# Attention's output kept as channel rows through HBM and divided per eight heads, with two expert weight loads moved into routing

## What is computed

```python
# layer 0, attention: 16 heads of width 16
Q, K, V = (proj(Wq, bq), proj(Wk, bk), proj(Wv, bv))         # [4, 16, 1024, 16]
scores = jnp.einsum('bhqd,bhkd->bhqk', Q, K) * scale
attn = softmax(scores, axis=-1)
out = jnp.einsum('bhqk,bhkd->bhqd', attn, V)
out = out.transpose(0, 2, 1, 3).reshape(B, S, D) @ Wo.T + bo
x = layernorm(x + out)
# layer 0, experts: top 2 of 8 by softmax(x @ w_gate.T), hidden width 1024
h = gelu(einsum('td,edh->teh', flat_x, W1) + b1)
y = einsum('teh,ehd->ted', h, W2) + b2
x = layernorm(x + sum of the two chosen experts, weighted)
```

## Time and profile before

| | us |
|---|---|
| median of 3 runs | 2013.42 (2012.56 to 2052.93) |
| the profiled execution, its own time | 2010.89 |
| its span, first to last instruction | 2008.9 |
| attention's loop over heads | about 104 to 897 |
| output projection | 899 to 942 |
| normalisation, gate, routing | 942 to 1015 |
| experts of layer 0 | 1016 to about 1580 |
| second layer | from about 1590 |

### The profile page before, as it was taken

The page is one execution under the profiler, slowest core; times in us unless marked ns, Lnnn a source line. Parts: engine busy times, 40 slices in busy tenths (PEclk is TensorE's granted clock), DMA queues, the critical chain, the costliest instruction groups (busy, mean ns, idle before and its releaser), DMA issues. The chain is left out here.

```text
span 2008.9 us, 36274 instructions
## 1 busy us (share of the span) xinstructions
PE 1763.1 (88%) x11202; PEld 1122.9 (56%) x11203; DVE 1146.1 (57%) x2473; ACT 887.8 (44%) x1306; POOL 408.6 (20%) x573
## 2 busy tenths in 40 slices
PE   7999999999999999988479999999999579944772
PEld 4523444444444444437368888888888546943551
DVE  4688888888888888846821111111111287797223
ACT  3436666666666666664112333333332144230223
POOL 2310000000000000003013333333333100000782
PEclk9969999999999999999789999999999879977896
DMA  5501111111111111106624443344344300024544
GB/s 196 181 18 36 36 32 32 32 32 34 35 34 32 32 32 33 35 23 201 228 86 117 101 116 104 109 110 110 111 105 114 93 6 1 2 84 147 87 54 168
DMA packets 101160, 157.44 MB, mean 78 GB/s; under 512 B 19984, under 2 KB 76624, under 8 KB 95728
## 3 DMA queue, kind: packets, MB, share of 16 engines
q1 hardware_dynamic: 70720, 120.30, 18.4%
q0 software_dynamic: 21696, 23.85, 7.5%
q10 hardware_dynamic: 8688, 12.58, 1.7%
HBM read 122.23 MB, written 48.37 MB: 85 GB/s over the span
## 5 line engine op out<-in xcount | busy, mean ns | idle before, releaser
L552 DVE TENSOR_REDUCE unit_max<-ps_ring 128x1 f32<-128x512 f32 x1024 | 639.3, 683 | 70.1 <-PE ps_ring L427 64.1
L538 ACT ACTIVATE w<-ps_scores 128x1024 f32<-128x1024 f32 x512 | 503.6, 1022 | 263.3 <-PE ps_scores L504 260.4
L427 PE MATMUL ps_ring<-k_stack,q_stack 96*128 96x512 bf16 x1024 | 367.6, 393 | 17.6 <-POOL v_padded L390 7.6
L504 PE MATMUL ps_scores<-q_stack,k_stack 98*128 98x512 bf16 x1024 | 307.5, 382 | 2.6 <-ACT w L538 2.5
L1486 PE MATMUL m_ps_h<-m_xt,m_w 128*128 128x256 f32 x1248 | 278.6, 382 | 0.8 <-DVE m_xt L1537 0.8
L1498 PE MATMUL m_ps_y<-w,m_ht 128*128 x1248 | 275.8, 379 | 0.0
L449 PE MATMUL ps_o<-w,v_padded 128*32 128x256 f32 x4096 | 261.9, 385 | 0.0
L1486 PEld LDWEIGHTS m_ps_h<-m_xt,m_w 128*128 128x128 f32 x1248 | 239.0, 192 | 34.2 <-DVE m_xt L1537 1.2
L1498 PEld LDWEIGHTS m_ps_y<-w,m_ht 128*128 128x128 f32 x1248 | 234.2, 190 | 30.3
L427 PEld LDWEIGHTS ps_ring<-k_stack,q_stack 96*128 96x128 bf16 x1024 | 98.8, 97 | 259.0 <-DVE unit_max L552 177.2
L1518 ACT ACTIVATE m_ht<-m_ps_h,m_w 128x256 f32<-128x256 f32 x312 | 130.7, 470 | 144.8 <-PE m_ps_h L1486 144.8
(11 more groups left out here) (263 smaller groups left out, 1624.2 us busy)
## 6 DMA issues: line engine op xcount, KB each, us to landing
m_w<-in_w SPq DMA_DIRECT2D x39, 1028.0 KB
rows<-g_rows SPq DMA_DIRECT2D x16, 512.0 KB, 3.0
y<-sums SPq DMA_DIRECT2D x16, 512.0 KB, 7.1
q_parts<-qk_part SPq DMA_DIRECT2D x16, 384.0 KB
k_parts<-qk_part SPq DMA_DIRECT2D x16, 384.0 KB
q_stack<-q_parts SPq DMA_DIRECT2D x64, 96.0 KB
k_stack<-k_parts SPq DMA_DIRECT2D x64, 96.0 KB
xt<-in_xt ACTq DMA_DIRECT2D x8, 512.0 KB, 10.0
```

Source lines behind the costliest of these rows:

```text
L427: nc.tensor.matmul(out[:, :], qs[0:STACK, u, qt * P:(qt + 1) * P], ks[0:STACK, u, half * HALF:(half + 1) * HALF], start=True, stop=True).t ...
L504: mm = nc.tensor.matmul(p_s[kt % 2][:, half * HALF:(half + 1) * HALF], ks[:, u, kt * P:(kt + 1) * P], qs[:, u, half * HALF:(half + 1) * HALF],
L538: nc.scalar.activation(pt[:, kt, :], p_s[kt % 2][:, :], ACT.Exp, scale=SCALE)\
L552: nc.vector.tensor_reduce(unit_max[:, u % 2, half, qt:qt + 1], src[:, :], axis=AX.X, op=ALU.max).then_inc(ring_used, 1)
```

## The change

1. In attention the fold is gone: no transposes back, no `normalise`, no `c.ao`. Each head's `o_transposed` (32 rows of 1024 queries) is stored to `o_raw` in HBM by SP (`store_o`, 128 KB). Before ACT writes `o_transposed` for head n it waits until the store of head n - 2 has landed.
2. Heads are grouped by eight: the first and last groups are written out, six between are a hardware loop. Per group, one group late, SP loads the raw rows of eight heads (512 KB) and their sums (`load_block`, at head 1), DVE takes 64 reciprocals per partition (after head 2), SP stores them to HBM (at head 3) and reads them back spread over the 16 channels of each head (512 KB, at head 4), and DVE multiplies 128 x 1024 values (`scale_block`, after head 5) into `c.o_t`, channels on partitions. At the end of each group two ring numbers are passed over, to keep the loop's bank numbers fixed.
3. The output weights, the bias and the tokens of sequence 0 are loaded near the end of attention, and POOL adds the bias to those tokens there.
4. `stage_output` reads `c.o_t` directly as the stationary operand: no staging, transposes or copies; four PSUM banks in place of two, four token buffers in place of two. The last block of eight heads is loaded, inverted, stored, loaded back and scaled in this stage, in DVE's list the reciprocal ahead of the first pair and the scaling ahead of pair 5; only pairs 12 to 15 need it.
5. The first weights of expert units 0 and 1 are loaded by SP in routing, as soon as DVE has the owners of the units (L1144), behind the copies to `sums`.

```diff
+def load_block(sp, c, g):
+    raw = c.o_raw[bass.ds(g * HEADS, HEADS), :, :]
+    sp.dma_start(c.raw[:, :, :].rearrange("p j f -> p (j f)"), raw[:, 0:HD, :]).then_inc(c.raw_loaded, 16)
+    sp.dma_start(c.den[:, :], raw[:, HD, :]).then_inc(c.den_loaded, 16)
+def store_reciprocals(sp, c, g):
+    sp.dma_start(c.o_inv[bass.ds(g, 1), :].rearrange("a (p f) -> (a p) f", p=P), c.rden[:, :]).then_inc(c.inv_stored, 16)
+def load_reciprocals(sp, c, g):
+    rows = c.o_inv[bass.ds(g, 1), :].rearrange("a (h f) -> (a h) f", h=HEADS).unsqueeze(1)
+    sp.dma_start(c.inv[:, :, :].rearrange("p j f -> p (j f)"), rows.to_broadcast([HEADS, HD, S])).then_inc(c.inv_loaded, 16)
+def scale_block(v, c, kb):
+    def split(x):
+        return x.rearrange("p j (b q) -> p j b q", b=2)
+    return v.tensor_tensor(c.o_t[:, bass.ds(kb, 1), :].rearrange("p a (b j q) -> p (a j) b q", b=2, j=4),
+                           split(c.raw[:, :, :]), split(c.inv[:, :, :]), ALU.mult).then_inc(c.scaled, 1)
...
# attention, order of heads and ring
-                if kt == FOLD_AT and u % 2 == 0 and not (first and u == 0):
-                    yield kt, "spare"
-                    yield kt, "fold"
+            if u == HEADS - 1 and not last:
+                for _ in range(SPARES):
+                    yield KT, "spare"
...
# attention, SP
-                    for u in range(SLOTS):
+                    for u in range(HEADS):
...
+                        if not first:
+                            if u == 1:
+                                for p in range(2):
+                                    sp.wait_ge(c.o_stored[p], g * (HEADS // 2 * 16))
+                                sp.wait_ge(c.scaled, g)
+                                load_block(sp, c, g)
+                            if u == 3:
+                                sp.wait_ge(c.inverted, g)
+                                store_reciprocals(sp, c, g)
+                            if u == 4:
+                                sp.wait_ge(c.inv_stored, g * 16)
+                                load_reciprocals(sp, c, g)
+                        if not (first and u == 0):
+                            store_o(n - 1, u + 1)
                         for j, (_, kind) in enumerate(units(first, last, u)):
                             if kind == "rows":
                                 rows((u + 1) % SLOTS, count_before(g, first, last, u) + j)
+                        if last and u == HEADS - 3:
+                            sp.dma_start(wo[:, :, :], a.wo.rearrange("(c p) n -> p c n", p=P)).then_inc(c.wo_loaded, 16)
+                            sp.dma_start(bo[:, :], a.bo.partition_broadcast(P)).then_inc(c.bo_loaded, 16)
+                            for h in range(2):
+                                sp.dma_start(xin[h][:, :, :], c.tokens[0, h, :, :, :]).then_inc(c.x_loaded[h], 16)
...
# attention, DVE
+                        if not first and u == 2:
+                            dve.wait_ge(c.den_loaded, g * 16)
+                            nc.vector.reciprocal(c.rden[:, :], c.den[:, :]).then_inc(c.inverted, 1)
+                        if not first and u == 5:
+                            dve.wait_ge(c.raw_loaded, g * 16)
+                            dve.wait_ge(c.inv_loaded, g * 16)
+                            scale_block(nc.vector, c, g - 1)
...
# output stage
+                for p in range(2):
+                    sp.wait_ge(c.o_stored[p], NH // 2 * 16)
+                sp.wait_ge(c.scaled, BLOCKS)
+                load_block(sp, c, BLOCKS)
...
+                sp.wait_ge(c.inverted, BLOCKS)
+                store_reciprocals(sp, c, BLOCKS)
+                sp.dma_start(w2[:, 0:FC, :], w2_experts[0]).then_inc(w2_loaded, 16)
+                sp.wait_ge(c.inv_stored, LAST)
+                load_reciprocals(sp, c, BLOCKS)
...
+                    wait_from(pe, summed, i - 3)
+                    pe.wait_ge(c.scaled, min(2 * b + 2, BLOCKS) + 1)
...
+                            mm = nc.tensor.matmul(p_y[i % 4][:, j * D:(j + 1) * D],
+                                                  c.o_t[:, 2 * b + k, t * P:(t + 1) * P],
                                                   wo[:, k, :], start=(k == 0), stop=(k == KC - 1))
...
+                dve.wait_ge(c.den_loaded, LAST)
+                nc.vector.reciprocal(c.rden[:, :], c.den[:, :]).then_inc(c.inverted, 1)
+                for i in range(NT // 2):
...
+                    if i == 5:
+                        dve.wait_ge(c.raw_loaded, LAST)
+                        dve.wait_ge(c.inv_loaded, LAST)
+                        scale_block(nc.vector, c, BLOCKS - 1)
...
# routing, SP
+                if first_weights is not None:
+                    wait_apart(sp, spare_sp, owned, 1)
+                    first_weights(sp)
```

More of the change, by code:

```diff
@@ L474, in body @@
                 def body(g, first, last):
-                    for u in range(SLOTS):
-                        n = g * SLOTS + u
-                        ahead = not (last and u >= 2)
+                    for u in range(HEADS):
+                        n = g * HEADS + u
+                        ahead = not (last and u >= HEADS - 2)
                         before = count_before(g, first, last, u)
@@ L702, in product @@
                                                   wo[:, k, :], start=(k == 0), stop=(k == KC - 1))
                     mm.then_inc(made, 1)
-                def pairs(b, first, last):
-                    for s in range(PAIRS):
-                        if not (last and s == PAIRS - 1):
-                            turn(b * PAIRS + s + 1, s + 1)
-                        product(b * PAIRS + s, s)
-                pe.wait_ge(loaded_w, 16)
-                turn(0, 0)
-                peeled_ends(pe, B, pairs)
@@ L970, in stage_gate, with stage_route @@
         mem.clear()
[L973 removed]
+def stage_route(nc, c, tiles, fixed, rows, sums, late_loads=None, wide=1, first_weights=None):
     with ExitStack() as stack:
```

318 lines of the change are left out of this document (144 added, 174 removed).

## The result

| | before | after |
|---|---|---|
| median, us | 2012.99 (2006.83 to 2052.93) | 1998.01 (1989.37 to 2004.37) |
| runs | 6 | 6 |
| ratio to before, 95% interval | | 0.9942 (0.9913 to 0.9970) |
| the profiled execution's span | 2008.9 | 1993.7 |

The changed kernel is faster by 0.6%, 11.7 us by the ratio, 15.0 by the medians. The 2052.93 of before is one slow execution, which the ratio leaves out. The forecast was 1975 with a range of 1966 to 1987: the time lies 11 us above its upper end, on the side of the rival "the loop over eight heads refetches its code", and 3 us beyond that rival's own 1980 to 1995.

The account below looks back on a forecast made before the run. PE bounds attention, in lockstep with DVE. Fold and tail 33.0, less multiplication 4.9, plus output stage 6.9 and experts' start 3.2, give 38.2 us off the 2013.42 median: 1975 predicted, range 1966 to 1987.

Parts of the forecast that it names:

- the loop over eight heads refetches its code: Rival, attention: PE's doubled body waits one landing at each of five jumps back, about 13 us, giving 1988; chance 0.13.
- The fold's removal: Attention: 30 folds of 1.06 us each vanish from the head periods, saving 31.7 us.
- the natural experiment: Attention: the trace before already alternates heads with a fold, 12.52 us, and without, 11.56, so it prices the fold.
- The tail: End of attention: head 62's fold saves 0.5 us, and the last fold behind the loop 0.8.
- The passage to the output stage: From ACT's last copy to the next stage's first DMA: 1.87 us becomes 1.0, so 0.8 saved.
- The multiplication: Attention, DVE, seven times behind L560: delays PE's fourth unit by 0.7 us each, costing 4.9.
- The reciprocal: Attention, DVE behind L560: 0.56 us, making DVE about 0.2 late, with 0.3 still free, so no cost.
- SP's row write: Attention, SP: shifts by up to 0.6 us, 1.2 more with load_block; 3.7 us of cover remain, so cost 0.
- the rival at 2055: Attention: SP's queue holds the row write over 3.7 us later, each head grows, 80 us lost against 38 gained; chance 0.03.
- The output stage: From 43.0 to 36.1 us, saving 6.9; bounds 33 without the stall, 40 with slower DMA legs and late tokens.
- output stage gives nothing: Rival: the HBM round trip or late tokens hold DVE until the stage takes 43 again, giving 1982; chance 0.11.
- The experts' start: PE's first expert transposes start 3.2 us sooner, the gather no longer beside two 1 MB loads; bounds 0 and 4.

Follow-up runs that it names:

- pool_scale: Against pe_loop4: in attention each block's multiplication is done by POOL in place of DVE; 1967.78 us, ratio 0.9781 to the kernel before.
- pe_loop4: Against after: PE's loop runs over four heads, the other engines' over eight, one ring number passed over per four heads; 1969.36 us, ratio 0.9798 to before.
- out_late_scale: Against after: the last block's multiplication stands ahead of pair 10 in place of pair 5 in DVE's output stage; 1999.56 us, ratio 0.9955 to before.
- before_body8: Against before: every engine's loop goes over eight heads, two groups of four per round, the fold stays; 2031.38 us, ratio 1.0110.
- out_order: Against after: SP asks for the sums ahead of the raw rows and for the 1 MB weights behind all tokens; 1995.79 us, ratio 0.9926 to before.
- out_act_queue: Against all_fixes: the last block's reciprocals go out and back through ACT's DMA queue, multiplication ahead of pair 9; 1965.42 us, ratio 0.9764 to before.
- all_fixes: pe_loop4 with the edits of out_late_scale and out_order added; 1972.43 us, ratio 0.9820 to before.

## Why the prediction was wrong, point by point

**The fold's removal: right.** Nearly all plain periods are 11.56 to 11.59, as the earlier trace rows had it for a head without a fold; the natural experiment carried over, with two such heads next to each other and eight. pool_scale, with neither folds nor multiplications in DVE's periods, has 61 periods in 705.9, 31.0 us under before's 736.9, for the 31.7 of the forecast. pe_loop4's are 27.8 shorter; the sum had 31.7 - 4.9 = 26.8.

**The tail.** The stretch from the last join to the end of the copy became 0.5 shorter: that is the fold of head 62, forecast at 0.5. The passage to the output stage, forecast to save 0.8, is part of the next point: SP's first issue there is 3.4 us behind the copy (893.2 to 896.6), because the last store must land first, for the 1.0 + 1.8 of the working.

**The multiplication: a little dear.** Forecast seven of 0.7, 4.9; measured six of 0.54 (periods 12.09 to 12.11), and the seventh falls where DVE reduces no more: 3.2. The reciprocal shows in no period, as argued. That it costs PE the whole excess was right, and pool_scale shows it by taking it away.

**SP's row write: right.** No period grew for it, and PE waits for no `q_stack` at the scores; the rival at 2055 has nothing in the trace.

**The refetch: the step that failed.** The sum has no term for the five jumps back of PE's loop; they cost 29.1 us, more than all that attention was to give. The refetch was seen and named as a rival, with its place, its number of jumps and its sign in the trace, all of which came true: five long periods, one per eight heads, with instruction packets beside them. Two things in it were wrong. The chance, 0.13: nothing in the profile of before said that a body of 1550 recorded instructions is held, only that one of 800 is. The Trainium skill ("Runtime: NRT & Kernel Launch", section "Instruction fetch mechanics") gives the rule that a taken branch outside the window stalls for a fetch, and the trace agrees; its figure of 2048 instructions for PE would have let the long body fit, and there the measurement decides: the chip fetched again. I had read this figure as evidence against the rival, and it was none for this loop.
And the price: 1.9 to 3.7 a jump, 13 us in all; measured 29.1. The landing time was a fair estimate of the stop itself, 3.1. What was missing is its consequence: PE is 98.6% busy in attention at clock 1.00 and behind each stop of 3 us it worked at 0.50 for 5.4 us. The price of a stop was taken as its length, and it was nearly twice that. With 29.1 in place of 13 the rival's own sum is 1975 + 29 = 2004, 6 us above the measured 1998, and with the 4.2 that the output stage fell short it is 2008. What makes up for it is the 8.9 us in stretches of the same code, which no term had. So that the rival's 1988 lies within 10 us of the time is in part luck.

**The output stage: mis-sized.** Forecast 6.9, with the 0.8 of the passage 7.7; measured 3.5. One wait in DVE's list was forecast at 1 to 3 us and is 5.2. By the forecast the spread reciprocals are there 1.0 + 16.5 = 17.5 us behind attention's last copy; it became 23.8 (916.94 - 893.19). Two terms were short. The sums were to land 3.7 us after the issue of their load and took 6.4 (897.98 to 904.34, the load issued behind that of the raw rows), and the spread reciprocals took 10.2 from the start of their load's issue to their use (906.77 to 916.94) where 6.5 were given. The prediction had seen both as "each DMA leg takes twice as long", and used it only for the range. DVE's pair was cheaper than thought, 1.38 for 1.60. But the bound was read at the wrong place: out_late_scale removed that wait and gained nothing, since the next, tokens that SP asks for late, stood right behind it. The case "output stage gives nothing" named late tokens, at 0.11; half of it came true.

**The experts' start: right.** 3.2 forecast; 3.4 in after, 4.8 where it is the only part made. 1.9 us from the gather's issue to PE, for 3 forecast. The wait itself thus fell by 4.3 and not by 3.2; the rest of after's stretch was 0.9 longer than before's, and the near hit is in part luck.

**What neither shows.** In the second layer, whose code is the same, the three kernels made from before took 415.5, 414.1 and 417.2 us, and the ten made from after 411.6 to 413.9. That is 2.7 us between the means and not explained here. It is no small part of the 11.7 us that the change gave, and it hides part of what the jumps cost.

## What to carry to other kernels

Before a hardware loop's body is made longer, read whether the instruction queue moves anything in that loop: where it moves nothing, the present body is held, and that says nothing of one twice as long. Change the grouping of the data and the grouping of the code apart, as pe_loop4 does: the same change was worth 2.0% with PE's loop over four heads, and 0.6% with it over eight. And where a stage rests on one queue's list, look at what stands behind a wait in that list before speeding up what is waited for.

## What the runs showed of the hardware

- A stop of PE of about 3 us, in work at clock 1.00, can be followed by the clock's lower level (0.50 for 5.4 us, at five jumps of five in after) or not (1.00 at four of six in before_body8, whose two stops read are 2.78 and 2.91). The first makes a stop of 3.1 cost 5.8.
- PE's loop body of about 800 recorded instructions is held over 13 jumps back, one of about 1550 is fetched anew at each: 2 packets of the instruction queue against 53 in 600 us, and 40 for the same list written out.
- A multiplication of two SBUF operands on DVE, 128 x 1024, took 1.21 us alone and 2.80 to 3.32 when it began during an addition on POOL; begun before one, it kept its 1.21 and POOL's addition took 2.77 and 3.31 in place of 2.35. Reductions from PSUM did not change (period 11.57) beside a multiplication on POOL of 2.36.
- The store of 32 KB took at most 1.5 us to land in after and 7.6 and 6.9 in out_order and out_act_queue, in the latter on another engine's queue than the loads. So having a queue of its own did not let it pass. In these three and in all_fixes SP or ACT went on to the load back 0.5 to 1.4 us behind the landing of the tokens asked for before the store, read from the start of POOL's first addition (905.33 and 906.77 in after, 907.38 and 908.80 in out_order, 879.64 and 881.06 in all_fixes, 882.18 and 882.66 in out_act_queue). In after the store was issued when those tokens had all but landed, in the others 6.5 to 6.8 us before. That fits a store that lands only with the loads in flight beside it; no run took the loads away.
